# Three rows of the query stack carry the negative maximum: attention in an eight-stage kernel on one Trainium2 core

## The reference, cut to what matters

```python
x = x + xattn_L0(layernorm(x), ctx, ...)     # A0: plain
x = x + ffn_L0(layernorm(x), ...)            # E0
x = x + xattn_L1(layernorm(x), ctx, ...)     # A1: with rotary positions
x = x + ffn_L1(layernorm(x), ...)            # F1
x = x + xattn_L2(layernorm(x), ctx, ...)     # A2: one key and value head shared by 16 query heads, biases
x = x + ffn_L2(...); x = x + xattn_L3(...); x = x + ffn_L3(...)
# each of A0, A1, A2, per head:
attn = softmax(q @ k.T / sqrt(8)); out = attn @ v; return out @ Wo.T
```

## Time and profile before

| what | us |
|---|---|
| median of 3 runs | 1900.86 |
| lowest and highest | 1881.29, 1918.4 |
| profiled execution, its own time | 1893.17 |
| its span, first to last instruction | 1891.4 |
| loops of A0, A1, A2 in the profile | 216, 235, 242 |

### The profile page before, as it was taken

How to read it: one execution, slowest core, us unless ns; L and a number is a source line. 1 busy time by engine, 2 the same in 40 slices (tenths; PEclk the granted TensorE clock), 3 DMA queues, 4 the chain that set the end, 5 groups by cost and what they waited for, 6 DMA issues and landing times. The chain is left out here.

```text
span 1891.4 us, 43279 instructions
## 1 busy us (share of the span) xinstructions
PE 1498.1 (79%) x14594; PEld 1225.4 (65%) x14607; DVE 1068.1 (56%) x3418; ACT 778.0 (41%) x1494; POOL 462.3 (24%) x546
## 2 busy tenths in 40 slices
PE   3899967999999999689999769779979965139910
PEld 1777756988889898367777327567757655139910
DVE  2677754434443434488888557558867767313322
ACT  1566633444444444245555435446623352014400
POOL 2233321101100001122222222223312123740066
PEclk9999987999999999689999869889989996569955
DMA  5765510000000000245543023232120031112222
GB/s 155 193 179 153 155 62 1 1 1 0 0 1 0 1 0 0 76 129 128 147 117 85 1 61 109 68 92 81 53 112 0 5 123 45 52 53 93 93 70 75
DMA packets 102114, 130.94 MB, mean 69 GB/s; under 512 B 10478, under 2 KB 82434, under 8 KB 95536
## 3 DMA queue, kind: packets, MB, share of 16 engines
q1 hardware_dynamic: 97912, 121.54, 22.9%
q0 software_dynamic: 4096, 8.07, 1.5%
HBM read 88.13 MB, written 41.77 MB: 69 GB/s over the span
## 5 line engine op out<-in xcount | busy, mean ns | idle before, releaser
L475 DVE TENSOR_REDUCE A_neg_max<-A_s_bank 128x4 f32<-128x512 f32 x408 | 272.2, 685 | 123.3 <-PE A_s_bank L570 115.1
L357 ACT ACTIVATE A_probsT<-A_st_bank 128x512 f32<-128x512 f32 x384 | 227.8, 599 | 114.1 <-PE A_st_bank L585 107.7
L583 PE MATMUL A_st_bank<-A_q_stack,A_k_stack 72*128 72x128 bf16 x1536 | 225.4, 224 | 23.2 <-issue 22.1
L1759 PEld LDWEIGHTS E_y_bank<-E_w,E_h 128*128 128x128 f32 x2048 | 237.8, 192 | 5.3
L1759 PE MATMUL E_y_bank<-E_w,E_h 128*128 128x128 f32 x2048 | 239.7, 275 | 0.0
L1656 ACT ACTIVATE E_h<-E_h_bank,w_L_b 128x512 f32<-128x512 f32 x260 | 173.0, 691 | 160.2 <-PE E_h_bank L1749 158.1
L585 PE MATMUL A_st_bank<-A_max_partsT,pick_head 96*128 96x128 bf16 x1536 | 224.9, 223 | 0.0
L583 PEld LDWEIGHTS A_st_bank<-A_q_stack,A_k_stack 72*128 72x128 bf16 x1536 | 156.3, 103 | 51.2 <-issue 49.5
L570 PE MATMUL A_s_bank<-A_k_stack,A_q_stack 72*128 72x128 bf16 x1632 | 166.2, 227 | 28.7 <-DVE A_neg_max L475 23.3
L1585 DVE SCALAR_TENSOR_TENSOR x_sb<-E_y_bank,E_gates,x_sb 128x128 f32 x256 | 72.0, 344 | 181.1 <-PE E_y_bank L1759 180.3
L585 PEld LDWEIGHTS A_st_bank<-A_max_partsT,pick_head 96*128 96x128 bf16 x1536 | 153.6, 100 | 12.2 <-issue 10.6
(11 more groups left out here) (270 smaller groups left out, 3054.5 us busy)
## 6 DMA issues: line engine op xcount, KB each, us to landing
A_q_stack<-q_scratch SPq DMA_DIRECT2D x51, 576.0 KB
A_k_stack<-k_scratch SPq DMA_DIRECT2D x34, 576.0 KB
q_scratch<-A_q_parts SPq DMA_DIRECT2D x54, 192.0 KB, 2.3
A_ctxT<-in_ctxT SPq DMA_DIRECT2D x39, 256.0 KB, 6.4
k_scratch<-A_k_parts SPq DMA_DIRECT2D x36, 192.0 KB
q_scratch<-A_q_parts SPq DMA_DIRECT2D x54, 128.0 KB, 2.2
slots_in<-F_zeros SPq DMA_DIRECT2D x10, 512.0 KB, 5.0
E_xe<-slots_in SPq DMA_DIRECT2D x40, 128.0 KB, 2.2
```

What stands on the lines that cost most here:

```text
L357: act.activation(probsT[n % 2][:, c * HQ:(c + 1) * HQ, :], st_bank[c % 2][:, :].rearrange("k (a q) -> k a q", a=HQ), ACT.Exp, scale=scale) ...
L475: dve.tensor_reduce(neg_max[:, c * HQ:(c + 1) * HQ], s_bank[c % 2][:, :].rearrange("q (a k) -> q a k", a=HQ), AX.X, ALU.max, negate=True). ...
L583: pe.matmul(dst, k_stack[slot][:, h % kheads, at:at + S], q_stack[slot][:, h, at:at + S], start=True, stop=False)
L1759: last = pe.matmul(y_bank[e % 2][:, j * D:(j + 1) * D], h[e % 2][:, f, j * S:(j + 1) * S], w2[:, e, f, :], start=(f == 0), stop=(f == FC - 1))
```

## The change

The stacks grow from 72 to 75 rows. The three new rows of `k_stack` are set to one by GpSimd ahead of everything else that it does in a stage (rows 64 to 74 are set, and the loads later write 64 to 71 over), and SyncE's first load waits for that. The three new rows of `q_stack` get the three parts of the negative maximum: after `copy_max`, ScalarE waits for its own copy and issues a transfer of 48 rows of 128 bf16 (12 KB) from `max_partsT` into 3 rows of 16 heads by 128 queries. `scoresT` is then one product of 75 rows per head, and the selection products go, with the `pick_head` constant, its load of 768 KB and its conversion. `scores` uses the first 72 rows, as before.

`scoresT(b, n, 0)` now waits for the transfer's semaphore in place of that of the copy. `transpose_max(b + 1)` moves from behind the third `scoresT` of a block to behind the first `scores`, and `copy_max(b + 1)` from behind the third `exps` to behind the first.

```diff
+WITH_MAX = COMBO + 3
-        q_stack = [sb(f"q_stack{i}", [COMBO, NH, HALF], BF16) for i in range(4)]
-        k_stack = [sb(f"k_stack{i}", [COMBO, kheads, HALF], BF16) for i in range(4)]
+        q_stack = [sb(f"q_stack{i}", [WITH_MAX, NH, HALF], BF16) for i in range(4)]
+        k_stack = [sb(f"k_stack{i}", [WITH_MAX, kheads, HALF], BF16) for i in range(4)]
...
+                    if isinstance(g, int) and g == 0 and half == 0 and step == 0:
+                        sp.wait_ge(ones_done, 4)
...
+            for n, t in enumerate(k_stack):
+                pool.memset(t[64:WITH_MAX, :, :], 1.0).then_inc(ones_done, 1)
+                pool.wait_ge(ones_done, n + 1)
             for t in v_pad:
...
-                act.copy(max_partsT[q][:, :], wo_bank16[0:96, 0:S]).then_inc(mt_copied, 1)
+                act.copy(max_partsT[q % 2][:, :], wo_bank16[0:96, 0:S]).then_inc(mt_copied, 1)
+                act.wait_ge(mt_copied, b + 1)
+                at = (q % 2) * S
+                act.dma_start(q_stack[q // 2 % 4][COMBO:WITH_MAX, :, at:at + S],
+                              max_partsT[q % 2][0:3 * NH, :])\
+                    .then_inc(max_loaded[q % 2], 16)
...
                     exps(b, n, 0)
+                    copy_max(b + 1, n + 1)
                     exps(b, n, 1)
                     place(0)
                     exps(b, n, 2)
-                    copy_max(b + 1, (n + 1) % 2)
...
-                own.link(dve.tensor_copy(max_parts[:, 32:32 + NH], max_r[:, :]))
+                own.link(dve.tensor_copy(max_parts[:, NH:2 * NH], max_r[:, :]))
...
                 if c == 0:
-                    pe.wait_ge(mt_copied, b + 1)
+                    pe.wait_ge(max_loaded[n % 2], PIECES * (4 * scores.it + n // 2 + 1))
...
-                    pe.matmul(dst, k_stack[slot][:, h % kheads, at:at + S], q_stack[slot][:, h, at:at + S],
-                              start=True, stop=False)
-                    last = pe.matmul(dst, core.pick_head[:, h, :], max_partsT[n % 2][:, :], start=False, stop=True)
+                    last = pe.matmul(st_bank[c % 2][:, a * S:(a + 1) * S], k_stack[slot][:, h % kheads, at:at + S],
+                                     q_stack[slot][:, h, at:at + S], start=True, stop=True)
...
                     scores(b + 2, n + 2, 0)
+                    transpose_max(b + 1)
                     scoresT(b, n, 1)
...
                     scoresT(b, n, 2)
-                    transpose_max(b + 1)
```

More of the change, by code:

```diff
@@ L161, in multi_head_attention @@
         mt_copied = sem("mt_copied")
+        max_loaded = [sem(f"max_loaded{i}") for i in range(2)]
+        ones_done = sem("ones_done")
         st_ready = sem("st_ready")
@@ L190, in multi_head_attention @@
         STACKED = 16 * 2
+        PIECES = 16
         def loop_of(eng):
@@ L229, in stack_half @@
                                     ap=[[span, 3 * DH], [step * DH * span, 3], [1, span]])
-                    sp.dma_start(dest[:, :, :].rearrange("r h t -> r (h t)"), three).then_inc(stack_loaded[slot], 16)
+                    if isinstance(g, int) and g == 0 and half == 0 and step == 0:
+                        sp.wait_ge(ones_done, 4)
+                    sp.dma_start(dest[0:COMBO, :, :].rearrange("r h t -> r (h t)"), three)\
+                        .then_inc(stack_loaded[slot], 16)
             def fetch(e, p):
@@ L418, in _ @@
             copy_out(NB)
+            act.wait_ge(max_loaded[0], PIECES * (NB // 2 + 1))
         @block.vector
@@ L484, in split_max @@
                 own.link(dve.tensor_tensor(max_r[:, :], neg_max[:, :], max_parts[:, 0:NH], ALU.subtract))
-                own.link(dve.tensor_copy(max_parts[:, 32:32 + NH], max_r[:, :]))
-                dve.tensor_tensor(max_parts[:, 64:64 + NH], max_r[:, :], max_parts[:, 32:32 + NH],
+                own.link(dve.tensor_copy(max_parts[:, NH:2 * NH], max_r[:, :]))
+                dve.tensor_tensor(max_parts[:, 2 * NH:3 * NH], max_r[:, :], max_parts[:, NH:2 * NH],
                                   ALU.subtract).then_inc(m_split, 1)
@@ L569, in scores @@
                     h = c * HQ + a
-                    last = pe.matmul(s_bank[c % 2][:, a * S:(a + 1) * S], q_stack[slot][:, h, at:at + S],
-                                     k_stack[slot][:, h % kheads, at:at + S], start=True, stop=True)
+                    last = pe.matmul(s_bank[c % 2][:, a * S:(a + 1) * S], q_stack[slot][0:COMBO, h, at:at + S],
+                                     k_stack[slot][0:COMBO, h % kheads, at:at + S], start=True, stop=True)
                 last.then_inc(s_ready, 1)
@@ L581, in scoresT @@
                     h = c * HQ + a
-                    dst = st_bank[c % 2][:, a * S:(a + 1) * S]
-                    pe.matmul(dst, k_stack[slot][:, h % kheads, at:at + S], q_stack[slot][:, h, at:at + S],
-                              start=True, stop=False)
-                    last = pe.matmul(dst, core.pick_head[:, h, :], max_partsT[n % 2][:, :], start=False, stop=True)
+                    last = pe.matmul(st_bank[c % 2][:, a * S:(a + 1) * S], k_stack[slot][:, h % kheads, at:at + S],
+                                     q_stack[slot][:, h, at:at + S], start=True, stop=True)
                 last.then_inc(st_ready, 1)
@@ L2216, in program @@
         core.ident16 = sb("ident16", [128, 128], BF16)
-        core.pick_head = sb("pick_head", [96, NH, S], BF16)
         core.rope_cos = sb("rope_cos", [D, S])
@@ L2286, in load_rest @@
                 sp.dma_start(dst, src).then_inc(rest_loaded, 16)
-        with nc.sbuf_tensor("wide_pick", [96, NH, S], F32) as wide_pick, nc.Block() as block:
-            first_loads.append((wide_pick[:, :, :], ap["pick_head"], "wide_pick"))
+        with nc.Block() as block:
             @block.sync
@@ L2312, in _ @@
                 dve.tensor_copy(core.ident16[:, :], core.ident[:, :])
-                dve.tensor_copy(core.pick_head[:, :, :], wide_pick[:, :, :])
         def convert_rest():
@@ L2357, in shape_constants @@
     c = {"ident": np.eye(128, dtype=np.float32)}
-    pick = np.zeros((96, 16, 128), np.float32)
-    for part in range(3):
-        for h in range(16):
-            pick[32 * part + h, h, :] = 1.0
-    c["pick_head"] = pick
     c["iota8"] = np.arange(8, dtype=np.float32).reshape(1, 8)
```

## The result

The changed kernel takes 2026.5 us (median of 4 runs, 2014.8 to 2035.9) where the kernel before took 1892.9 (4 runs, 1881.3 to 1918.4): 1.073 times as long, 95% interval 1.061 to 1.084. I had forecast 1869, in a range to 1910, from a median of 1900.9; a fourth run of before has moved that to 1892.9. The profiled execution took 2035.92 us; its span is 2034.9, 143.5 more than before's.

A forecast was written before the change was run, and what follows sets the result against it. It took A0's short block to be a ring through all engines ending at VectorE's split, and VectorE to bound A1. Loops -36, returns -27, start -4, ones +27, first transfers +8 gave -32: 1869 us, own range 1846 to 1890, with rivals 1834 to 1910.

The forecast's parts named there:

- The transfer: Maxima into `q_stack`: 2.6 us with the issue, hidden in the loops, bare once ahead of each: 8 us lost.
- lands late: Rival: transfer beside stack loads takes 6.4 us, TensorE waits at `scoresT` 0, about 4 us a group, 1965 us; chance 0.12.
- The clock: TensorE's clock in the loops: left out of the forecast, taken to stay at 0.99 of full speed.
- Products removed: 1536 selection products, 0.06 us each on TensorE: 3.84 us a group, 92 us in all, gross.
- The transposition moved: TensorE waits for VectorE's split at the earlier place: about 0.4 us across a block's end, 1.35 us beside GpSimd's subtraction.
- gross gain: TensorE time of the removed products before any waits: 0.96 us a block, 3.84 a group, 92 us in all.
- the bound of A1: VectorE bounds A1's loop, waiting only 12.8 us for scores; gain there capped at that, taken as 8 us.
- Ones: GpSimd's four settings ahead of the layer norm's root: 13.2 us lost in A0, 14.2 in A1, 27 together.
- The loop's return: A2's loop: with a shorter body both late returns vanish, 13.6 us each, 27 us saved.
- Start and first transfers: Ahead of the loops: dropped 768 KB load gains 4 us at the start; bare first transfers lose 8 us.
- The range: Forecast's own range of whole time, from bounds for loops and ones, without the rivals' bounds: 1846 to 1890 us.

The follow-up runs named there:

- x_bare: The kernel before without the 16 selection products of a block (maximum left out of the softmax), nothing else changed: 1873.7 us, 0.986 of before.
- y_move: The kernel before without selection products, with transposition of the maxima and ScalarE's copy at the new, early place; no transfer, no ones: 1938.9 us, 1.032 of before.
- x_nowait: The changed kernel with its transfer issued but neither read nor waited for by the transposed scores (maximum left out of the softmax): 1982.6 us, 1.045 of before.
- y_issue: The kernel before without selection products, ScalarE issuing the transfer each block, unread; transposition and copy at the old place, no ones: 1917.5 us, 1.019 of before.
- y_bare_twice: The kernel before without selection products, each transposed score product issued twice, transposition at its old place: 1894.9 us, 1.014 of before.
- x_quarter: The changed kernel with each stack load cut in four, so packets are 2 KB instead of 8 KB: 1967.0 us, 1.049 of before.

## Why the prediction was wrong, step by step

The spans differ by 143.5 us, and the traces divide them. The loops together: before 673.7, x_bare 642.8, y_move 698.9, x_nowait 716.0, after 770.0. So removing the products gave 30.9 (27 of them the late returns), the early place cost 56.1, the issue with the ones in place 17.1, the landing 54.0; outside of the loops 47.2 were lost (11.7 ahead of A0, 18.6 ahead of A1, 2.7 ahead of A2, 14.2 behind). The price of a step is the one that it has in this order; y_issue shows that another order gives others.

I had forecast the loops 63 us shorter (36 and the returns' 27), and they are 96 longer. Of these 159 us, 71 are the transfer (landing and issue). The other 88 are the removal with the early place: I had them at -63, and they measured +25. So two steps failed, and each is told below.

**The transfer: the first step that failed.** I took 2.6 us to the landing, hidden. Without loads ahead it is so; behind them it was up to 12.8, and TensorE waited 69.6 us for it. The rival "lands late" had the mechanism and its place, but from the wrong row: 6.4 us, in a queue of its own, and a chance of 0.12. Its 4 us a group stands against 54 / 24 = 2.3 measured in the loops. Alone it would have made 1869 + 54 = 1923 us, under the 1939 from which I called it slower by 2%; only with the issue's 17 does the transfer reach that line. The issue was taken at 0.36 us, from SyncE's row, with 0.5 of cover; it is 0.74.

**The clock, left out: part of the second failure.** I took 0.99 to stay, since TensorE would be "asked for less by some 10%, not left idle". It fell to 0.77 and 0.81; with only the products gone, already to 0.89 in A1. What that cost is seen by the doubled products in A1 alone, 8 and 9 us given back, net of what the products themselves take. The early place's price stays when the clock is kept up; for the landing and the issue no run parts the waits from the clock.

**Products removed: the second step that failed.** The pitch of 0.06 us held, but it is not what a block gives back. Without any other step A0 gave 10.4 us of 30.7, and A1 less than nothing.

**The transposition moved.** The wait of 1.35 us was measured at 1.41. My allowance in A0, 1.75 a group, would be 42 us for 24 groups and so near the 56 that y_move measured, but I set it against a gross gain that was not there. VectorE did not stay the bound of A1: it waited 12.8 us for scores there, but 25.5 us in x_bare, which has fewer products and nothing else new, and 56.3 us in after.

**Ones.** 27 us forecast; hiding them gave back 11.2 and 11.6, 23 in all. Right, by elements as taken, and a little too dear. Some 7 us more were lost ahead of A1; y_move and y_bare_twice, without ones, lose as much there (563 and 562 us), and x_bare does not, so what makes them stays open.

**The loop's return.** Both returns are on time, as forecast. But 27 us as a gain of the change was a misreading: I took for a property of the kernel what one execution showed, and that this term came true in the two traces is in part luck.

**Start and first transfers.** A0 starts at 13.63 instead of 16.66, 3.0 us (4 taken); the first transposed scores stand 2.7 us behind the copy (2.6). Right.

**The rest.** Behind the last loop after is 14.2 us longer, but x_bare, without transfer or ones, is 9.7 longer there too, and x_quarter only 3.3. It goes with the chip and not with the change: in all runs on two of the chips (eight traces) this stretch is 519 to 523 us long, in all on the two others (ten) 529 to 533; before's trace has 519.3, after's 533.5. Why the chips differ stays open.

**The range.** Its own bounds, loops 0 to 60 us and ones 13 to 27, added up give 1831 to 1905, not the 1846 to 1890 that I wrote. It made no difference, since no bound on the loops allowed a loss.

## What to carry to other kernels

A small transfer that an engine waits for should be priced by what stands on the DMA engines at that time, whoever issued it; here bulk loads cut into packets of 2 KB brought its longest landing from 12 us to 4. Taking products off TensorE gave back a third of their time in the best loop and less than nothing in another, where it left idle time and the clock fell. And a step that is moved earlier in a ring should be moved no further than its input is ready: half way instead of all the way was worth 52 us.

## What the runs showed of the hardware

- A transfer of 12 KB in pieces of 256 bytes landed 12.8 us after its issue behind loads in 8 KB packets, and in 3.3 us (4.0 at most) behind the same loads in 2 KB packets. Spreading it from 3 to 16 engines by three transfers left the waits at 71.0 us against 69.6.
- Behind 8 KB packets nothing of it moved for 6 us, and then mostly one piece on an engine for each packet of 8 KB, 0.5 to 0.6 us apart.
- 512 redundant products made a loop shorter, 260 to 240 us in one trace each, with the granted clock going from 0.81 to 0.96.
- The late return of A2's loop (9.5 to 13.5 us) came 1 to 3 times of 3 in four traces of equally long bodies.
- GpSimd set 11 x 4096 bf16 four times in 14.20 us, and the same bytes as 11 x 2048 float32 in 7.43.
- ScalarE's issue of a transfer holds it for 0.74 us, twice what SyncE's shortest takes (0.36).
